# Scores of attention two once, in full precision: VectorE subtracts the maximum, TensorE transposes

## The reference

```python
x = x + _L0_conv_ref(_gn(x), ...)     # attention one: 8 heads, position bias
x = x + _L1_conv_ref(_gn(x), L1_conv_w_qkv, L1_conv_w_out)   # attention two
...
qkv = flat @ w_qkv.T                  # H = 16 heads of HD = 16
k_cat = jnp.concatenate([k_prev, k], axis=2)    # own chunk and the one before
scores = jnp.einsum('bclhd,bcmhd->bchlm', q, k_cat) * scale
scores = jnp.where(valid[None, :, None, None, :], scores, jnp.finfo(scores.dtype).min)
attn = jax.nn.softmax(scores, axis=-1)
out = jnp.einsum('bchlm,bcmhd->bclhd', attn, v_cat)
```

## Time and profile before

| | us |
|---|---|
| median of three runs | 181.91 (181.73 to 183.41) |
| the profiled execution | 181.56 |
| its span, first to last instruction | 179.8 |
| PE busy | 160.8 |
| VectorE busy | 140.9 |
| ScalarE busy | 103.3 |
| POOL busy | 84.1 |

### The profile page before, as it was taken

The page is one execution under the profiler, slowest core; times in us unless marked ns, Lnnn a source line. Parts: engine busy times, 40 slices in busy tenths (PEclk is TensorE's granted clock), DMA queues, the critical chain, the costliest instruction groups (busy, mean ns, idle before and its releaser), DMA issues.

```text
span 179.8 us, 3978 instructions
## 1 busy us (share of the span) xinstructions
PE 160.8 (89%) x1434; PEld 123.0 (68%) x1434; DVE 140.9 (78%) x356; ACT 103.3 (57%) x225; POOL 84.1 (47%) x106
## 2 busy tenths in 40 slices
PE   0789679899989997999799999999999999999973
PEld 0289569778867786789668657777667876666551
DVE  1494878988794889687999899888989779888130
ACT  3103698578666764868575774757555684344420
POOL 0915439525624372512396286624484359455000
PEclk9999999999999999999999999999999999999999
DMA  4549300000000000000000000000000000100101
GB/s 116 195 137 344 106 0 5 0 0 4 2 0 0 5 0 2 4 0 0 0 0 4 0 0 7 0 4 0 0 33 29 4 0 29 33 2 25 37 10 52
DMA packets 4979, 5.34 MB, mean 30 GB/s; under 512 B 440, under 2 KB 4920, under 8 KB 4960
## 3 DMA queue, kind: packets, MB, share of 16 engines
q1 hardware_dynamic: 4496, 4.80, 8.2%
q10 hardware_dynamic: 464, 0.28, 0.7%
HBM read 4.02 MB, written 1.06 MB: 28 GB/s over the span
## 4 chain that ended last, share of the span: by engine, by line
PE 69%; DVE 17%; issue 5%; ACT 5%; DMA 2%; POOL 1%; DVEq 0%; POOLq 0%
PE bank L567 14%; PE bank L510 6%; PE bank L543 5%; PE bank L623 5%; PE bank L614 4%; PE bank L660 4%; PE bank L529 4%; PE bank L564 4%; PE bank L555 4%; DVE bank L882 4%; DVE bank L904 3%; PE bank L519 3%; ACT QM L1080 2%; PE bank L551 2%; PE bank L656 2%
## 5 line engine op out<-in xcount | busy, mean ns | idle before, releaser
L1101 ACT ACTIVATE PT<-bank 128x512 f32<-128x512 f32 x64 | 38.3, 601 | 42.7 <-PE bank L567 22.6
L343 POOL TENSOR_TENSOR Qk<-Qn,con 128x512 f32<-128x512 f32 x32 | 37.1, 1164 | 27.3 <-PE bank L567 26.9
L882 DVE CUSTOM_DVE_ANT_0 bank<-bank,Tk 128x256 f32<-128x256 f32 x64 | 25.8, 446 | 9.9 <-PE bank L529 9.9
L567 PE MATMUL bank<-Qk,Kf 128*128 128x512 f32 x64 | 32.6, 591 | 0.0
L894 DVE TENSOR_TENSOR D<-con,NM 128x512 fp32r<-128x512 f32 x32 | 28.9, 903 | 2.0 <-PE bank L567 1.9
L319 POOL TENSOR_TENSOR D<-con,NM 128x256 fp32r<-128x256 f32 x32 | 19.6, 620 | 20.0 <-PE bank L555 16.6
L886 DVE TENSOR_REDUCE NM<-bank 128x4 f32<-128x512 f32 x32 | 21.9, 683 | 1.9 <-PE bank L543 1.8
L904 DVE TENSOR_TENSOR bank<-bank,Tk 128x512 f32<-128x512 f32 x32 | 23.2, 725 | 0.0
L529 PE MATMUL bank<-KH,QM 128*128 128x256 f32 x64 | 15.1, 319 | 4.6 <-ACT QM L1080 4.6
L543 PE MATMUL bank<-Km,Qs 128*128 128x512 f32 x32 | 16.6, 520 | 0.0
L555 PE MATMUL bank<-QM,KL 128*128 128x256 f32 x64 | 16.5, 280 | 0.0
(11 more groups left out here) (136 smaller groups left out, 325.6 us busy)
## 6 DMA issues: line engine op xcount, KB each, us to landing
Tk<-bias_rows SPq DMA_DIRECT2D x4, 384.0 KB, 4.7
X<-x SPq DMA_DIRECT2D x4, 256.0 KB, 4.7
y<-Y SPq DMA_DIRECT2D x8, 128.0 KB, 1.7
Kf<-w_qkv SPq DMA_DIRECT2D x1, 768.0 KB, 7.8
Kf<-w_outb SPq DMA_DIRECT2D x1, 256.0 KB, 7.9
con<-consts ACTq DMA_DIRECT2D x1, 145.5 KB, 2.8
PT<-w_qk ACTq DMA_DIRECT2D x1, 128.0 KB, 4.4
PT<-buckets SPq DMA_DIRECT2D x1, 64.0 KB, 3.1
```

The source lines that it names most:

```text
L343: nc.gpsimd.tensor_tensor(Qk[:, idx % QRING, :].rearrange("p (a v q) -> p v a q", a=4, v=2), Qn[:, b % 2, g, c * CHUNK:(c + 1) * CHUNK].un ...
L567: return nc.tensor.matmul(z[:], Kf[:, b % 3, g, w:w + 2 * CHUNK], Qk[:, (b * BLK + u) % QRING, :], start=False, stop=True, skip_group_chec ...
L882: last = V.tensor_tensor_reduce(half, half, Tk[:, u, nt * P:nt * P + CH], 1.0, LOWEST, ALU.add, ALU.max, NM[:, i % 2, 2 * u + nt:2 * u + n ...
L1101: A.activation(PT[:, u, :], bank[Z_BANK + u % 2][:], ACT.Exp, scale=SCALE).then_inc(p_ready, 1)
```

## The change

In attention two the scores are made once, and `Km`, `Qs` are plain float32. VectorE takes the maximum as before and right behind it subtracts it from the scores, from PSUM to a ring of four tiles `SBB` in SBUF (`below_max`). `shifted_b` then transposes those four 128 x 128 squares into Z_BANK. Gone are the diagonals of attention two, the product with `minus` there, the second score product and POOL's `head_queries`. The score bank is released by the subtraction, no longer by the maximum. `Kf` is one plain copy, `Qn` and `Kf` have one buffer each, and the window of keys of a chunk is an access pattern with steps in place of repeated columns. Weights are staged in a tile of their own, no longer in `Kf`.

```diff
-        Km = sb("Km", [P, 2, 4, TOK], F32R)
+        Km = sb("Km", [P, 2, 4, TOK])
...
-        Qs = sb("Qs", [P, 2, 2, NCH, 2, CHUNK], F32R)
-        QRING = 3
-        Qk = sb("Qk", [P, QRING, BW])
+        Qs = sb("Qs", [P, 2, 2, NCH, 2, CHUNK])
...
+        BRING = 4
+        SBB = sb("SBB", [P, BRING, BW])
...
-                if c == 0:
-                    rhs = keys[:, :, 0:CHUNK].unsqueeze(2).to_broadcast([P, 4, 2, CHUNK])
-                else:
-                    rhs = keys[:, :, (c - 1) * CHUNK:(c + 1) * CHUNK]
-                return nc.tensor.matmul(bank[S_BANK + u % 2][:], Qs[:, b % 2, g, c].rearrange("p v q -> p (v q)"), rhs,
+                first, step = ((0, 0), (0, CHUNK), (2 * CHUNK, -CHUNK), (2 * CHUNK, CHUNK))[c]
+                window = bass.AP(keys.tensor, keys.offset + first, [keys.ap[0], [TOK, 4], [step, 2], [1, CHUNK]])
+                return nc.tensor.matmul(bank[S_BANK + u % 2][:], Qs[:, b % 2, g, c].rearrange("p v q -> p (v q)"), window,
                                         start=True, stop=True)
...
             def shifted_b(i, u):
 
                 z = bank[Z_BANK + u % 2]
-                b = i - BATCH
-                c, g = u // 2, u % 2
-                nc.tensor.matmul(z[:], minus[:], D[:, (i * BLK + u) % DRING, :], start=True, stop=False, skip_group_check=True)
-                pe.wait_ge(qk_ready, b * BLK + u + 1)
-                w = WINDOW[c] * CHUNK
-                return nc.tensor.matmul(z[:], Kf[:, b % 3, g, w:w + 2 * CHUNK], Qk[:, (b * BLK + u) % QRING, :],
-                                        start=False, stop=True, skip_group_check=True)
+                below = SBB[:, ((i - BATCH) * BLK + u) % BRING, :]
+                for a in range(4):
+                    last = nc.tensor.transpose(z[:, a * P:(a + 1) * P], below[:, a * P:(a + 1) * P], ident)
+                return last
...
-                if idx >= 2:
+                if idx >= BATCH * BLK + 2:
+                    pe.wait_ge(sub_ready, idx - BATCH * BLK - 1)
+                elif idx >= 2:
                     pe.wait_ge(max_ready, idx - 1)
...
-            def diagonal(i, u):
+            def below_max(i, u):
 
-                idx = i * BLK + u
-                n = 4
-                dve.wait_ge(max_ready, idx + 1)
-                dve.wait_ge(z_done, idx - DRING + 1)
-                V.tensor_tensor(D[:, idx % DRING, 0:n * P].rearrange("p (h q) -> p h q", h=n),
-                                con[:, C_ID:C_ID + P].unsqueeze(1).to_broadcast([P, n, P]),
-                                NM[:, i % 2, n * u:n * u + n].unsqueeze(2).to_broadcast([P, n, P]), op=ALU.mult).then_inc(d_ready, 1)
+                idx = (i - BATCH) * BLK + u
+                dve.wait_ge(max_ready, i * BLK + u + 1)
+                if idx >= BRING:
+                    dve.wait_ge(z_done, i * BLK + u - BRING + 1)
+                V.tensor_tensor(SBB[:, idx % BRING, :].rearrange("p (h m) -> p h m", h=4),
+                                bank[S_BANK + u % 2][:].rearrange("p (h m) -> p h m", h=4),
+                                NM[:, i % 2, 4 * u:4 * u + 4].unsqueeze(2).to_broadcast([P, 4, P]), op=ALU.subtract).then_inc(sub_ready, 1)
...
             for t in range(STEPS):
-                ahead = t - LAG + AHEAD
-                if BATCH * BLK <= ahead < UNITS * BLK:
-                    diagonal(ahead // BLK, ahead % BLK)
                 if t < UNITS * BLK:
                     block_max(t // BLK, t % BLK)
+                if BATCH * BLK <= t < UNITS * BLK:
+                    below_max(t // BLK, t % BLK)
```

More of the change, by code:

```diff
@@ L204, in build @@
         stat_step = sem("stat_step")
-        s_done, max_ready, da_ready, d_ready = (sem(n) for n in ("s_done", "max_ready", "da_ready", "d_ready"))
-        km_ready, qk_ready = sem("km_ready"), sem("qk_ready")
+        s_done, max_ready, da_ready, sub_ready = (sem(n) for n in ("s_done", "max_ready", "da_ready", "sub_ready"))
+        km_ready = sem("km_ready")
         zb_ready, qm_ready = sem("zb_ready"), sem("qm_ready")
@@ L359, in window_values @@
                 pool.wait_ge(grs_ready, b + 1)
-                if ahead < BATCH * BLK:
-                    pool.wait_ge(da_ready, ahead + 1)
-                else:
-                    pool.wait_ge(qk_ready, ahead - BATCH * BLK + 1)
+                pool.wait_ge(max_ready, ahead + 1)
                 nc.gpsimd.tensor_copy(VB[0:CHUNK, n, 0, :, 0:HD], VB[0:CHUNK, n, 1, :, 0:HD]).then_inc(vx_ready, 1)
@@ L584, in shifted @@
                 else:
-                    pe.wait_ge(d_ready, idx - BATCH * BLK + 1)
-                if u == 0:
-                    pe.wait_ge(k_ready if is_a(i) else kh_ready, i + 1)
+                    pe.wait_ge(sub_ready, idx - BATCH * BLK + 1)
+                if u == 0 and is_a(i):
+                    pe.wait_ge(k_ready, i + 1)
                 if idx >= 2:
@@ L804, in queries_keys @@
                         for v in range(2):
-                            last = V.tensor_scalar(Qs[:, b % 2, :, :, v, :], Qn[:, b % 2].rearrange("p g (c q) -> p g c q", c=NCH),
+                            last = V.tensor_scalar(Qs[:, b % 2, :, :, v, :], Qn[:].rearrange("p g (c q) -> p g c q", c=NCH),
                                                    con[:, C_HALF + v:C_HALF + v + 1], None, ALU.mult)
@@ L875, in block_max @@
                 elif i >= 2:
-                    dve.wait_ge(d_ready, (i - 2 - BATCH) * BLK + u + 1)
+                    dve.wait_ge(sub_ready, (i - 2 - BATCH) * BLK + u + 1)
                 if is_a(i):
@@ L1059, in projected @@
                         act.wait_ge(q_done, i + 1)
[L1060 to L1062 removed]
+                        if b:
+                            act.wait_ge(q_ready, i)
+                        A.activation(Qn[:].rearrange("p g n -> p (g n)"), f[:], ACT.Copy).then_inc(qh_ready, 1)
                     if which == 2:
                         act.wait_ge(k_done, i + 1)
[L1065 to L1071 removed]
+                        if b:
+                            act.wait_ge(km_ready, 2 * b)
+                        A.activation(Kf[:].rearrange("p g n -> p (g n)"), f[:], ACT.Copy).then_inc(kh_ready, 1)
             def head_queries(i, u):
@@ L1089, in head_keys @@
                 for a in range(4):
-                    last = A.activation(Km[:, g, a, :], Kf[:, b % 3, g, CHUNK:CHUNK + TOK], ACT.Copy,
+                    last = A.activation(Km[:, g, a, :], Kf[:, g, :], ACT.Copy,
                                         scale=con[:, C_QUAD + a:C_QUAD + a + 1])
```

37 lines of the change are left out of this document (5 added, 32 removed).

## The result

The changed kernel takes **183.43 us** (median of 20 runs, 183.03 to 185.1), the kernel before 181.97 (20 runs, 181.37 to 185.07): a ratio of **1.008**, 95% interval 1.0049 to 1.011. That is inside the range given and within the one per cent called no change, but on the slow side of it: +0.8% where +0.2% was forecast, and the interval leaves out no change at all. The profiled execution took 183.28 with a span of 181.5, that is 1.72 more than the one before (181.56).

The account below looks back on a forecast made before the run. PE was taken as the bound, with waits for VectorE: +0.8 +1.0 +0.5 +0.5 −0.6 −1.7 = +0.5 (+0.4 unrounded) on 181.56, giving 182.0 profiled and a median of 182.3 us. Range 180.2 to 184.3.

Parts of the forecast that it names:

- PE bounds, its work unchanged: Attention two: PE is the bound, and its work per block goes only from 1.32 to 1.30 us.
- Subtraction 0.69, bounds 0.68 and 0.73: VectorE's new subtraction of the maximum from scores in PSUM takes 0.69 us, priced from neighbour rows L904 and L928.
- Heads +1.0 and +0.5, step 61 +0.5: PE waits longer for VectorE: +1.0 us in steps 39 to 41, +0.5 in 47 to 49, +0.5 for ON at 61.
- the walk: Operations set in their engine queues with durations from the rows and 0.04 us per semaphore, to find PE's waits.
- Tail −1.7: Scores of 63 to last shift: four cheaper shifts give −2.6 us, less waits of 0.5 at step 64 and 0.4 at 68.
- Entry +0.8: Steps 32 to 36: PE gets 2.5 us more, of which 1.6 falls into waits; bounds 0 and 2.5.
- the walk of before: The same queue walk for the unchanged kernel; at the entry it found about 2.9 us of waits for agg, ON, mom, XTl.
- block by block: PE over 32 blocks of attention two: 1.30 against 1.32 us each, −0.6 in all.
- The bank hold: Rival, slower: scores wait until VectorE's subtraction frees their bank, 184.0 us, or 184.9 with contended norm steps; 22%.
- The slack is 0.08.: Bare steps: bank hold 2.52 us against PE's 2.60 per two steps; a subtraction from 0.77 on makes scores wait.
- the waits close: Rival, faster: norm steps freed of POOL finish in time, no head waits and the entry hides wholly, 179.0 us; 15%.
- transposes don't overlap: Rival: four transposes end to end take 1.09 us, 0.65 more than counted, 32 times: +21, 203 us; 3%.

Follow-up runs that it names:

- experiment 7: Kernel before with Km and Qs as plain float32, so its maximum-only scores are full precision too; the rest of the old shift stays: 200.16 us, ratio 1.0946.
- experiment 6: Changed kernel with one more unused 128 x 128 VectorE instruction between maximum and subtraction of every block: 183.97 us, ratio 1.0094 to the kernel before.
- edits 1 and 2: Changed kernel with norm steps ahead of the subtraction (1) and attention two's value rows copied by ScalarE, not VectorE (2): 182.53 us; 2 alone 182.34.
- edit 1: Changed kernel with the norm steps dev, gm and mom of attention two moved ahead of the subtraction at unit heads: 182.55 us, ratio 1.0015 to the kernel before.
- experiment 5: Changed kernel with POOL given one unused 128 x 512 multiplication of constants per block: 183.41 us, ratio 1.0047 to the kernel before.
- the rounded kernel: Changed kernel with Km and Qs in the rounded format, so scores take 0.23 instead of 0.86: 173.26 us, and 173.47 on another chip.
- experiment 4: Changed kernel making scores for only half of the heads (256 of 512 columns) in blocks 32 to 35: 182.56 us, ratio 1.0031 to the kernel before.

## Why the prediction was right, and what was mis-sized

**PE bounds, its work unchanged: shown.** 1.29 a block against 1.32; the time goes with PE's work (experiment 7: 20.2 more, 18.0 later) and hardly with VectorE's (experiment 6: subtractions delayed by 2.6 in sum, 0.6 later). Accordingly 10 us off VectorE and 38 off POOL were worth nothing.

**Subtraction 0.69, bounds 0.68 and 0.73: 0.692.** The neighbour rows with one operand in PSUM gave it.

**Heads +1.0 and +0.5, step 61 +0.5: +0.7, +0.45, +0.35.** Same places, same waits, somewhat shorter. At the head of unit 5 the walk had 0.7, 0.5 and 0.3. The first two stand in the trace with these brackets, and measured from where PE would have been ready they are 0.67 and 0.46; the third, ahead of L474, is 0.19 without a bracket. Together that is 1.3 of the 1.5.

```profile
108.65 0.38 PE L471 MATMUL bank<-agg,con 128*128 128x2 f32 x2 [0.52 <-DVE agg L828]
...
109.25 0.44 PE L626 MATMUL bank<-con,ON 128*128 128x128 f32 x2 [0.22 <-DVE ON L890]
```

**Tail −1.7: −1.76.** "t2 at step 64 waits 0.5 for ON" is the 0.37 below; the give-back before t1 is the 0.79 from the last transposes to L619, where 0.44 would be free.

```profile
167.66 0.44 PE L626 MATMUL bank<-con,ON 128*128 128x128 f32 x2 [0.37 <-DVE ON L895]
...
170.79 0.66 PE L541 MATMUL bank<-con,SBB 128*128 128x128 f32 x4
171.58 0.66 PE L619 MATMUL bank<-con,OS 128*128 128x128 f32 x4
```

**Entry +0.8: +1.94. This is the mis-sized term.** The step that failed is "the walk of before finds about 2.9 in the four waits of this stretch", of which the longer scores were to fill all but 1.3. The first number was wrong: it is 2.0 by my sum, 1.0 by the brackets, and three waits, not four. XTl got shorter without POOL (0.68 for 0.94), but PE had not waited for it here. `mom` had no POOL beside it in step 33, since POOL's first head query starts at 90.79, in step 34; `gnb` and XTl did, and were still shorter than at the later heads. That the walk's prices account for the rest of the 0.9 is my reading; no run tests it. So 0.5, not 1.6, of the 2.5 that PE gained fell into waits. The value lay inside the bounds 0 and 2.5, just short of the "over 2" that was to prove the forecast wrong. With 1.9 in its place, and the −0.3 that block by block came to, the sum is 1.9 + 0.7 + 0.45 + 0.35 − 0.3 − 1.75 = +1.35, which is the 1.34 of the table; the load's 0.39 makes it 1.73. That the time fell into the range is in part luck: the entry was 1.1 too small, and the heads were 0.5 too large.

**The rivals.** The bank hold (22%, 184.0 to 184.9) gave a time nearer to the measured one than the forecast did, for a reason that the list of waits and experiments 1 and 6 reject. Its "The slack is 0.08." is wrong, since "two steps with nothing else in them" don't occur: any two neighbouring steps hold t1, t2 or another product of PE. At steps 56 to 58 the subtraction of 56 is through at 152.76 and the scores of 58 begin at 153.08, 0.32 later. That the waits close (15%) did not happen by itself: it takes edits 1 and 2, and they bring 1.1 each alone and 1.4 together. Its sum takes off 1.6 for the heads, though the forecast had added 2.0 there, and gives no reason. That transposes don't overlap (3%) is excluded by 0.44.

**Open.** Whether the change with edit 1 is slower than the kernel before at all: 1.0015 with an interval on both sides of 1. What the norm's steps would cost if all of them met POOL: experiment 5 slowed `gnb` alone. And why the granted clock falls behind the waits of a head in some runs of the rounded kernel and not in others: no experiment was made on it.

## What to carry to other kernels

When two products are exchanged for others, first count PE at start-to-start distances: here +20 and −21 us of large steps cancelled, and what was left to predict was which engine's queue stands ahead of PE at a few heads. In a walk through a stretch, price every small operation by the row at that very place, with the neighbour engines that are at work there; waits taken from such a walk, with prices from other places, put the entry 1.1 too low. An instruction inserted in an in-order queue costs what it delays and is waited for, not its own length: records of 9.1 us delayed by 2.6 and cost 0.6, while moving three tiny operations ahead of one 0.69 operation brought 1.1. So measure from start to start what an experiment has added before reading its time.

## What the runs showed of the hardware that was not expected

- `gnb`, a 128x2 operation on SBUF, took 0.15 with POOL idle and from 0.46 to 1.02 in six places beside one of POOL's 128x512 multiplications (three in the kernel before, three in experiment 5). In all six it ended 0.05 to 0.07 after POOL's next multiplication started: it lasted until the one beside it was through. So the delay isn't fixed; it depends on when in POOL's 1.0 the operation starts. One of the six, in experiment 5:

```profile
93.34 1.02 DVE L859 SCALAR_TENSOR_TENSOR gnb<-gm,grs 128x2 f32<-128x2 f32 x1
...
94.30 1.05 POOL L340 TENSOR_TENSOR Idle<-con 128x512 f32<-128x512 f32 x1
```

- On VectorE the subtraction that reads the maximum starts 0.72 after it; an instruction that needs nothing of the maximum starts 0.60 after it, so that one of 0.28 put between the two delays the subtraction by 0.08 (experiment 6).
- A full-precision product on 256 columns is 0.43 shorter than on 512 (experiment 4), half of 0.86.
- Four transposes of 128 columns in float32, one record each, start 0.11 apart on average, 0.44 for 512 columns, beside 0.86 for one full-precision product on 512 columns in two records.
